# An expert part cut into tiles of 256 rows instead of 384

## The reference

```python
def gnn(x, adjacency, eps, W1, b1, rms_w, W2, b2):      # hidden size 512
    agg = eps * x + einsum('bnm,bmd->bnd', adjacency, x)
    h = silu(rmsnorm(agg @ W1 + b1, rms_w))
    return h @ W2 + b2

def ffn(x, Wg, bg, W1, b1, W2, b2):                     # 8 experts, hidden size 512
    scores, idx = top_k(x @ Wg.T + bg, 2)               # two experts per token
    probs = softmax(scores)
    return sum over both experts e of probs[e] * (relu(x @ W1[e].T + b1[e]) @ W2[e].T + b2[e])

x = x + gnn(layernorm(x), adj, ...)
x = x + ffn(layernorm(x), ...)
```

## Time and profile before

| | before |
|---|---|
| median of 3 runs | 847.71 us (844.83 to 849.97) |
| span of the profiled execution, first to last instruction | 833.8 us |
| around the span, up to the median | 13.9 us |
| TensorE busy | 649.5 us, 78% |
| VectorE / ScalarE / POOL busy | 437.2 / 363.1 / 471.8 us |
| mean granted TensorE clock | 0.911 |
| first scatter of the expert part | at 478.69 us |

### The profile page before, as it was taken

One profiled execution on the slowest core, in us unless ns is written; L12 is line 12 of the kernel. 1 busy time (PEld: TensorE's weight loads), 2 busy tenths in 40 slices (PEclk: granted clock), 3 DMA queues, 4 the chain that ended last, 5 costly groups with the idle time before them and its releaser, 6 DMA issues. The chain is left out here.

```text
span 833.8 us, 15678 instructions
## 1 busy us (share of the span) xinstructions
PE 649.5 (78%) x4143; PEld 577.3 (69%) x4144; DVE 437.2 (52%) x1376; ACT 363.1 (44%) x852; POOL 471.8 (57%) x477
## 2 busy tenths in 40 slices
PE   2799988887978779878855677888978789778880
PEld 2577767666767677767744677777867778777870
DVE  2569777775776657765645333433534334334340
ACT  3285755646556365563543332333333333333330
POOL 4314665455664555635475056676676755766765
PEclk9899998998998989989985799999999998999996
DMA  8943441244322443134513556576565755666733
GB/s 290 301 168 115 139 140 48 93 139 139 132 69 77 139 139 112 52 114 128 165 52 106 202 138 139 129 158 142 132 153 132 155 137 129 148 138 127 163 41 28
DMA packets 75267, 109.37 MB, mean 131 GB/s; under 512 B 8124, under 2 KB 54760, under 8 KB 75240
## 3 DMA queue, kind: packets, MB, share of 16 engines
q1 hardware_dynamic: 49544, 90.62, 33.0%
q0 software_dynamic: 25696, 18.43, 15.8%
HBM read 53.41 MB, written 26.02 MB: 95 GB/s over the span
## 5 line engine op out<-in xcount | busy, mean ns | idle before, releaser
L936 POOL DMA_INDIRECT out<-adj_in,goes x150 | 232.5, 1550 | 137.4 <-issue 77.8
L872 POOL DMA_INDIRECT slots<-rows,dest x128 | 127.4, 995 | 43.4 <-issue 37.8
L795 ACT ACTIVATE adj_in<-adj_in,share 128x128 f32<-128x128 f32 x150 | 49.5, 394 | 225.6 <-issue 121.9
L676 ACT ACTIVATE adjT_hi<-ps_t 128x512 fp32r<-128x512 f32 x128 | 76.1, 595 | 90.5 <-PE ps_t L478 71.9
L979 DVE TENSOR_TENSOR adjT_lo<-ps_t,adjT_hi 128x512 fp32r<-128x512 f32 x128 | 88.2, 690 | 49.7 <-ACT adjT_hi L676 45.3
L1170 DVE CAST goes<-adj_in 128x3 int32<-128x3 f32 x50 | 8.8, 175 | 197.3 <-DMA out<-adj_in,goes 176.1
L589 PE MATMUL ps_y<-W2s,siluT 128*128 128x128 f32 x512 | 76.6, 317 | 25.9 <-issue 20.2
L589 PEld LDWEIGHTS ps_y<-W2s,siluT 128*128 128x128 f32 x512 | 72.6, 229 | 27.5 <-issue 21.6
L478 PE MATMUL ps_t<-ident,adj_in 128*128 128x128 f32 x512 | 80.5, 282 | 13.9 <-POOL adj_in L858 13.3
L478 PEld LDWEIGHTS ps_t<-ident,adj_in 128*128 128x128 f32 x512 | 67.2, 147 | 32.2 <-issue 15.6
L471 PE MATMUL ps_agg<-adjT_hi,xn_hi 128*128 128x512 f32 (+1 forms) x152 | 71.7, 472 | 18.0 <-DVE adjT_lo L979 10.0
(11 more groups left out here) (174 smaller groups left out, 1365.0 us busy)
## 6 DMA issues: line engine op xcount, KB each, us to landing
adj_in<-in_adj SPq DMA_DIRECT2D x16, 2048.0 KB
W1cur<-W1e SPq DMA_DIRECT2D x26, 512.0 KB
adj_in<-slots SPq DMA_DIRECT2D x50, 196.5 KB
xn_hi<-W1e SPq DMA_DIRECT2D x12, 512.0 KB
xn_lo<-W1e SPq DMA_DIRECT2D x12, 512.0 KB
out<-x_all SPq DMA_DIRECT2D x16, 256.0 KB
adj_in<-biases SPq DMA_DIRECT2D x50, 66.0 KB
out<-adj_in,goes POOLq DMA_INDIRECT x150
```

Source lines behind the costliest of these rows:

```text
L676: act.activation(adjT_hi[m % 2][:, :], ps_t[m % 2][:, :], ACT.Copy).then_inc(s_hi, 1)
L795: ins = act.activation(ye[ku][:, j, :], yb[ku % 2][:, j, :], ACT.Copy, scale=share[ku][:, j:j + 1])
L872: pool.indirect_dma_start(out=slots, out_offset=bass.IndirectOffsetOnAxis(ap=dest[1 - par][:, c, j:j + 1], axis=0), in_=rows[1 - par][:, c ...
L936: pool.indirect_dma_start(out=out, out_offset=bass.IndirectOffsetOnAxis(ap=goes[ku][:, j:j + 1], axis=0), in_=ye[ku][:, j, :], in_offset=N ...
```

## The change

One constant is changed. All sizes that follow from it change with it.

```diff
--- before.py
+++ after.py
@@ -28,7 +28,7 @@
 ACT = mybir.ActivationFunctionType
 AX = mybir.AxisListType
 P = 128
-TILE = 384
+TILE = 256
 
 
 def build(nc, x, adj, eps, W1, b1, rms_w, W2, b2, Wg, bg, F1, fb1, F2, fb2, out):
```

## The result

| | before | after |
|---|---|---|
| median of 4 runs | 846.65 us (844.83 to 849.97) | 868.62 us (862.21 to 869.93) |
| ratio | 1 | 1.028 [1.023, 1.033] |
| span of the profiled execution | 833.8 us | 868.1 us |
| mean granted TensorE clock | 0.911 | 0.915 |
| first scatter into `out` | 478.69 us | 487.14 us |

The change makes the kernel 22 us slower, as forecast in sign, where 40.6 were forecast. (The median before has one run more than the 847.71 above.) The spans differ by 34.3 us, more than the medians do. The gap comes from the part that the change leaves alone. The last scatter into `slots` of the kernel before began at

What follows compares the result with a forecast made beforehand. A ring of waits from scatter landings through VectorE's cast back to POOL's scatters was taken to bound the expert part. Stage +44.5, last scatters -1.9, start -2.0: +40.6 on 833.8, with 13.9 around it 888 us, range 868 to 916.

Steps and rivals of the forecast that it cites:

- the ring through VectorE's cast: Expert part: VectorE's cast waits for landings, delaying bias, scaling and the scatter two tiles on; 13.36 us a pair, 10.64 after.
- One scatter less in a pair, 1.86: POOL, expert part: two scatters a tile instead of three take 1.86 us off each pair of tiles.
- VectorE 0.56 and ScalarE 0.30: Expert part, per pair: 128 fewer columns save VectorE 0.56 us in four instructions; one scaling less saves ScalarE 0.30.
- The landing doesn't depend on the tile's size: Expert part: the time from the scatters' end to their landing, 2.0 to 2.4 us, changes by 0.
- Seven first tiles at 1.5 us: Tiles 4 to 68: each expert's first tile waits for the tile before it, 1.5 us each, 10.5 in all.
- Tiles 0 to 4 26.9, and 68 to 70 10.4: Both ends of the scatter stage: 26.9 us for tiles 0 to 4, 10.4 for tiles 68 to 70.
- The start, -2.0, and the last scatters, -1.9: Outside the stage: TensorE's work until tile 0's result shrinks by 2.0 us, the last tile's own scatters by 1.9.
- 13.9 us around the span: Whole kernel: the timed median, 847.7, lies 13.9 us above the profiled span, 833.8; the same was added to the forecast.
- TensorE's busy share near 0.65: Expert part: a sign that the prediction is right, TensorE busy for near 0.65 of the stage.
- B: Rival, TensorE in the expert part: its clock falls and it becomes the bound, 913 to near 985 us; chance 0.08.
- C: Rival, expert part: more weight copies lengthen every landing to 3.0 us from 2.2, +30, 918 us; chance 0.14.
- D: Rival, expert part: the pace follows rows or scatters, -14.8 and the start's -2, so faster, 831 us; chance 0.04.

Runs made afterwards that it cites:

- t256_need_first: The changed kernel (256 rows), with POOL reading the number of earlier adds before it waits for the tile's result, not after; 772.5 us, 1.008 of the kernel before.
- t384_again: The kernel before (384-row tiles), unchanged, run once more for a second trace; 764.5 us, ratio 0.997.
- t256_goes_last: The changed kernel (256 rows), with VectorE's cast of the destinations moved from the start to the end of its step; 714.24 us, 0.933 of the kernel before.

## Why the prediction was right in sign and 19 us too high

1. *What bounds the kernel: the ring through VectorE's cast.* Shown. With the cast behind the step's work the stage falls from 370.2 to 299.9 us at 256 rows and from 340.4 to 306.0 at 384. A shorter step at another place of the ring (`t256_need_first`) shortens it; half the weights' traffic hardly does.
2. *One scatter less in a pair, 1.86.* Measured 1.86. This is the largest term, and it held.
3. *VectorE 0.56 and ScalarE 0.30.* The instructions were sized right. L1190's durations (least, median, most, in ns) are, before and then after:

```profile
L1190 DVE TENSOR_SCALAR hb<-ps_h,adj_in x25: 617/618/619, 469.6 to 806.0; 128x384 f32<-128x384 f32 x25
```

```profile
L1190 DVE TENSOR_SCALAR hb<-ps_h,adj_in x36: 482/484/486, 479.6 to 847.6; 128x256 f32<-128x256 f32 x36
```

   618 - 484 = 134 ns, for which 0.14 us stood, and L795's run went from 0.99 to 0.70. What the sum lacked are two places where I had no term. From the start of the second relu to that of L1197 the mean fell by 0.23 (0.73 to 0.50), the median by 0.13: in some turns L1197 is held up there by TensorE's second layer (L640). Between tiles 4 and 46 before, that happened seven times, between tiles 4 and 68 after, four times, and L1197 then starts 0.2 to 3.1 us after a stretch at the low level of the clock (1.2 GHz) has ended. One such stretch of before (columns as in the earlier trace rows; the granted clock is 0.53), and the L1197 behind it:

```profile
688.00:695.00 7.00, 6.02 (x21) 5.60 (x22) 5.06 (x17) 2.39 (x7) 3.46 (x3) 0.53 0.40 64
```

```profile
697.10 0.56 DVE L1197 TENSOR_TENSOR adj_in<-ps_g,adj_in 128x384 f32<-128x384 f32 x1 [2.12 <-PE ps_g L640]
```

   And L795's end to the scatter fell on average from 1.83 to 1.77 (1.73 to 1.58 in the turns shown), where 0 stood; why was not tested. With them the two stretches gave -0.53 and -0.49 for -0.42 and -0.44.
4. *The landing doesn't depend on the tile's size.* Wrong in a small way. The wait ends when the last scatter of a tile has landed, 2.20 us after its issue ended with three scatters in a tile, 1.97 with two, 2.35 with four. The prediction named this as what would make it wrong; the -0.28 of a clean pair is its largest missing piece. The number of scatters is not the whole cause: with the cast behind the step's work the landings are 2.06 to 2.24 with two, 1.90 with three and 2.11 with four. What sets them stays open. Together with point 3 it made a pair fall by 3.17 and not by 2.72, 0.45 more, or 14 us in 32 pairs. By luck part of this was hidden: the 13.36 that the sum starts from was 0.19 under the mean of before, so the pair was 10.38 where 10.64 stood, 32 x 0.26 = 8.3 us.
5. *Seven first tiles at 1.5 us.* In proportion the term most mis-sized. From tile 4 to 68 it took 336.04 = 32 x 10.38 + 3.9, so 0.56 each. I took the price from one stretch of before, with the pair's 13.36 from tiles 4 to 12 under it; the mean pair there is 13.55, and the same first tiles cost 8.2 / 8 = 1.0. At 256 rows they cost less still, since neighbouring tiles drift to about 5.2 us from each other (5.34, 4.97, 5.39 in a row), so that waiting for the tile just before, 6.0 to 6.9 (8.0 to 9.0 before), adds little to a distance that is made up within the pair. That is argued from these distances; no run tests it. This is 10.5 - 3.9 = 6.6 us.
6. *Tiles 0 to 4 26.9, and 68 to 70 10.4.* 26.70 and 9.70. With 4 and 5 the stage was 372.4 and not 388.3.
7. *The start, -2.0, and the last scatters, -1.9.* -3.4 and -2.8. With the stage's +28.7 for +44.5 that is the +22.4 of the traces where +40.6 stood.
8. *13.9 us around the span.* Wrong as a reading, and without effect on the sum. The profiled execution of the changed kernel took 869.81 us for a span of 868.1, so 1.7 lie around it, as in `t384_again`. The one of before was then some 11 us faster than the median, most likely in its first part, where its trace is 11.9 us ahead. A profile's span and a median of other executions can't be subtracted to give an overhead.
9. *TensorE's busy share near 0.65.* This sign missed: it is 0.79. The profile counts 296.05 / 71 = 4.2 us of TensorE's work a tile, and the prediction had 3.6. It is still under the 5.2 us that a tile takes.
10. *The rivals.* B is refuted as a bound: the granted clock was 0.95 in the stage. That mean hides short falls; between the levels 1 and 0.5 it stands for about a tenth of the stage at the low one (0.94 and an eighth before). They cost little, as point 3 shows. TensorE waited 34 times for VectorE's low part there, up to 2.5 us. The Trainium skill (page "TensorE: Matmul & The Clock Gate", section "HAM oscillation — how this bites in real kernels") describes bursts of matmuls that fall back to the half clock at every wait, but in its example the waits are of 3 to 5 us. The waits here are shorter, and the clock did not fall at each of them; the page's own case isn't tested by this trace. The value taken for 256 columns was right; these two rows (start and length) stand three matmuls apart, 0.35 / 3 = 0.117 us for each:

```profile
521.46 0.28 PE L471 MATMUL ps_h<-adjT_hi,W1cur 128*128 128x256 f32 x1
...
521.81 0.28 PE L471 MATMUL ps_agg<-adjT_hi,W1cur 128*128 128x256 f32 x1
```

C is refuted: landings became shorter, 2.9 at most (tile 1's; 3.24 before), at a DMA share of 0.66. D gave 831 if the pace followed the scatters. It did not with this order, but POOL's scatters do set the pace once the cast is moved: `t256_goes_last` has 4.28 us a tile on average, under the 4.97 from which on D counts, and is faster. D's own sum isn't confirmed by that: it has -14.8 in the stage for the smaller tile, and between the two kernels with the cast moved the stage differs by 6.1.

## What to carry to other kernels

When a ring of waits sets the pace, work out per turn what shrinks with the tile and what doesn't (here 3.4 of 10.4 us were the scatters, while the landing, the hand-overs and the register read nearly stayed), and only then choose the tile: a smaller one pays for the fixed part more often. Before that, look whether the wait that closes the ring has to stand where it stands. An instruction that waits for a slow transfer at the head of an in-order engine's step holds everything behind it, and moving it behind the step's work was worth 74 us here where the size was worth 22.

## What the runs showed of the hardware

- The landing of a tile's accumulating indirect scatters, counted from the end of the last one's issue, is about 2 us. With the cast ahead it is 1.97 and 1.98 us with two scatters (2.05 with POOL's read moved), 2.14 and 2.20 with three, 2.35 with four; with the cast behind, where POOL hardly pauses, 2.06 to 2.24 with two, 1.90 with three, 2.11 with four. So it doesn't simply grow with their number. Half the weights' traffic changed it by 0.04.
- POOL starts such scatters 1.855 us apart at a DMA share of 0.82 as at 0.62.
- TensorE's granted clock fell to its low level for a few us now and then in the stage, in both traces of either kernel, and VectorE's bias (L1197) was held up behind most of these falls, by 0.2 to 2.1 us.
- The part before the scatter stage, whose instructions are the same in all these kernels but for the sizes that follow from the tile, differed by 67 to 97 us between sessions (first scatter at 478.69 and 411.66, 487.14 and 409.31, 501.43 and 404.20 in traces of the same kernels). In the kernel before, between 20 and 380 us, the longer one shows TensorE pausing before L589 for nothing that the profile names, and VectorE before L1084, an addition for the scatters' places, for something that the profile doesn't hold (`remote`),

```profile
DVE place L1084 <- remote: 40.7, 10, 4.5
...
PE ps_y L589 <- issue: 20.2, 9, 5.4
```

  while `t384_again`, in a shorter one, has neither row. In the changed kernel's trace of the longer session the first is there as well (44.5 us from 20 to 400), and the second is 5.6. The granted clock from 100 to 300 us is 1.00 in `t384_again` and 0.91 to 0.93 in the trace before. The cause is open. It was not tested.
